# Compacting the heads' values by small transfers, and taking two groups of maxima ahead, in a decoder block

## The chip, the cores and the metric

The kernel runs on one core of a Trainium2 chip, as one launch. The metric is device time in microseconds (us), from the first to the last instruction and what lies around them. Matrix products run on TensorE (PE in the profile), vector work on VectorE (DVE), table functions and copies on ScalarE (ACT), some vector work on GpSimd (POOL); SyncE (SP) issues nearly all transfers.

## The reference

For four batches of 1024 tokens of width 256: self attention with 16 heads of width 16, whose queries and keys are made from 128-wide latents and rotated parts; a residual sum and layer norm; cross attention of the 1024 tokens with a context of 154 tokens under a mask; a residual sum and layer norm; then a routing layer with 8 experts of hidden width 512, each of which takes the best 256 tokens of every batch; last a layer norm. Cut to the attention and what follows it:

```python
attn = softmax(einsum('bhqd,bhkd->bhqk', query, key) / scale)
out = einsum('bhqk,bhkd->bhqd', attn, value)            # 16 heads of width 16
x = layernorm(x + out.transpose(0, 2, 1, 3).reshape(b, s, 256) @ Wo + bo)
# the same with the context as key and value, masked, W3 in Wo's place
x = layernorm(x + cross @ W3.T + b3)
probs = softmax(einsum('bsd,ed->bse', x, choice_w))     # 8 experts
```

## The kernel before

The time runs batch by batch. A batch has five stages: the self attention; its **out stage** (heads' values turned and divided, output projection, residual sum, layer norm, and then the query projection of the cross attention); the **operands** of the next batch's self attention; the **cross attention**; and its out stage, which ends in the logits of the routing (8 columns per token). A loop runs this body three times, and the fourth batch follows behind the loop without the parts for a next batch. The self attention of the first batch stands before the loop. After the fourth batch the experts run.

**Attention.** Heads go in groups of two, so there are eight groups. For each group three things happen. First the maxima: a product of 128 queries with all keys lands in two banks of PSUM and one VectorE reduction over it (`maximum`) gives the maximum. There are 16 of these per group of the self attention, 4 per group of the cross attention. GpSimd splits the negated maxima into three bfloat16 parts (`split_max`), PE turns them into rows (the order's step `turn`), ScalarE copies these (`nmT`), and SP moves them by three transfers into three extra rows of the queries' operand (`load_minus_max`). Second the scores (`st`): one product per 128 keys and 512 queries with keys in the rows, which subtracts the maximum through the extra rows, and one `Exp` on ScalarE. Third the weighted sum of values (`av`): up to four products side by side in one bank, four (head, half) pairs in 32 rows each. Column 17 of the values is 1, so row 16 of each 32 holds the sum of the exponentials. ScalarE copies the finished bank of a group into a slice of `oT`.

The order of these steps on every engine is a list written by `schedule` (`ORDER_SELF`, `ORDER_CROSS`, ...), one list for all engines: TensorE, VectorE and ScalarE each walk it and do their own part, in order. `ORDER_AHEAD` is the cross attention's list with the first 16 maxima of the next batch's self attention added (`ahead`, one after each `st` once the cross attention's own maxima are issued); `ORDER_NEXT` is the next self attention's list without them. The maxima use banks 0 to 3 in two pairs, so the product of one waits for the reduction two before it.

**The out stage** before: `o_tiles` turns `oT` (32 transposes), `heads_out` takes the reciprocal of the sums of every token and multiplies (8 reciprocals and 16 multiplications), `turn_heads` turns the result back (16 transposes) into `xT`, and `output` makes the projection (32 instructions, line L1568). `residual_sum` and `normalise` on VectorE, and a power on GpSimd, make the layer norm in two halves. In the self attention's out stage PE makes the `latents` of the next batch (L1409, 16 instructions) between the projection and the transposes of the normalised tokens (L1401); in the cross attention's it makes `context_values` (L1606 to L1616) there. `xTf`, the next batch's input, lies in the room of the keys before. Products that are copied out are handed on in a list of items (`Plan`), which also fixes their PSUM bank.

SP's program is a list too: in the loop's body it loads x, stores and reloads the split queries and keys, moves minus-maxima, and after the cross attention reloads the second half of the query stack, loads the mask, stores and reloads the context's parts, loads the residual and stores the normalised tokens (`x_rows`), before the next self attention's first minus-maxima.

## Time and profile before

| | us |
|---|---|
| median of 3 runs | 1962.59 (1958.56 to 1962.68) |
| the profiled execution | 1959.72 |
| its span | 1957.9 |

Busy over the span: PE 1668.1 us (85%), PE's weight loads 848.3, DVE 1134.5 (58%), ACT 891.8 (46%), POOL 429.8 (22%). The mean granted clock of TensorE was 0.907 of full speed.

How to read it: a row of the timeline has the start, the length, the engine, the source line, output and input by the program's names, the shape, and the count; in brackets behind it how long the engine had been idle and what released it. [...]

### The profile page before, as it was taken

The page shows a single profiled execution, that of the slowest core. Times are in us where ns is not written, and L with a number is a line of the kernel's source. Part 1 is how long each engine was busy: PE and PEld are TensorE (multiplying, and loading weights), DVE is VectorE, ACT ScalarE, POOL GpSimd, SP SyncE. Part 2 cuts the span into 40 slices and gives each one's busy share as a digit, 9 for nine tenths or more (in the row PEclk, how much of TensorE's full clock was granted, in tenths as well). Part 3 has the DMA queues.
Part 4 walks back from the last instruction along what each step waited for, and adds up shares of the span by engine and source line. Part 5 has one row for each costly group of instructions (what it writes and reads, how often), then busy time and mean ns, then how long its engine had stood idle before and what let it go on. Part 6 is the DMA issues. An engine that isn't in the chain of part 4 may idle for free. (4 is left out here: it accounts for less than half of the span.)

```text
span 1957.9 us, 32981 instructions
## 1 busy us (share of the span) xinstructions
PE 1668.1 (85%) x10632; PEld 848.3 (43%) x10632; DVE 1134.5 (58%) x1939; ACT 891.8 (46%) x1585; POOL 429.8 (22%) x547
## 2 busy tenths in 40 slices
PE   6599988798999888989998798999967844999993
PEld 3033334444332445433324354333245433888883
DVE  5577725756777256567763665677435366333424
ACT  2077773342777534347774343577833300111112
POOL 5200004302000052020001611100031001555563
PEclk9599999897999988979998899799988955999997
DMA  6700003622000044220000632200003040335446
GB/s 187 163 2 1 2 25 87 163 48 71 2 2 2 27 127 134 49 59 2 2 2 27 164 98 53 54 2 2 2 21 78 2 150 28 75 77 107 77 89 193
DMA packets 98037, 120.07 MB, mean 61 GB/s; under 512 B 17180, under 2 KB 73500, under 8 KB 97820
## 3 DMA queue, kind: packets, MB, share of 16 engines
q1 hardware_dynamic: 85468, 97.13, 18.1%
q0 software_dynamic: 12416, 20.98, 5.7%
q8 instruction: 86, 1.41, 0.3%
q14 instruction: 67, 0.55, 0.1%
HBM read 80.30 MB, written 40.79 MB: 62 GB/s over the span
## 5 line engine op out<-in xcount | busy, mean ns | idle before, releaser
L881 ACT ACTIVATE pT<-banks 128x512 f32<-128x512 f32 x1184 | 645.2, 596 | 254.8 <-PE banks L1492 150.0
L1034 DVE TENSOR_REDUCE nmf<-banks 128x1 f32<-128x1024 f32 x512 | 606.0, 1220 | 173.5 <-PE banks L1442 171.6
L1492 PE MATMUL banks<-qst,kst 99*128 99x512 bf16 x1024 | 344.0, 388 | 12.1 <-DVE nmf L1034 6.3
L1442 PE MATMUL banks<-kst,qst 96*128 96x512 bf16 x1024 | 327.0, 404 | 31.9 <-DMA kst<-k_parts 21.8
L1524 PE MATMUL banks<-pT,V 128*32 128x512 f32 x2048 | 273.8, 606 | 20.6 <-ACT oT L872 14.0
L1492 PEld LDWEIGHTS banks<-qst,kst 99*128 99x128 bf16 x1024 | 96.0, 97 | 307.2 <-ACT pT L881 185.8
L703 POOL CAST nmp<-nmf 128x16 bf16<-128x16 f32 x64 | 12.7, 198 | 831.4 <-DVE nmf L1034 516.6
L944 ACT ACTIVATE kst<-banks 128x512 f32<-128x512 f32 x64 | 38.2, 597 | 287.0 <-PE banks L1747 278.6
L1442 PEld LDWEIGHTS banks<-kst,qst 96*128 96x128 bf16 x1024 | 98.6, 100 | 146.4 <-DVE nmf L1034 37.3
L1029 DVE TENSOR_REDUCE nmf<-banks 128x4 f32<-128x616 f32 x128 | 99.6, 797 | 86.6 <-PE banks L1436 79.7
L1053 DVE RECIPROCAL rz<-banks 128x16 f32<-128x16 f32 x64 | 16.1, 251 | 204.5 <-PE banks L1552 203.4
L1277 DVE TENSOR_SCALAR kst<-banks,gate 128x256 f32<-128x256 f32 x64 | 28.0, 479 | 169.3 <-issue 164.6
L777 POOL DMA_INDIRECT acc_rows<-kst,tok_s x64 | 103.5, 1617 | 101.6 <-issue 97.7
L889 ACT ACTIVATE nmT<-banks 6x1024 bf16<-6x1024 bf16 x64 | 64.7, 1011 | 128.2 <-PE banks L1476 127.9
L1760 PE MATMUL banks<-qst,kst 128*128 128x256 f32 x512 | 120.8, 390 | 0.0
L1433 PE MATMUL banks<-maskb,identb 128*128 128x308 bf16 x256 | 79.3, 322 | 45.6 <-DVE V L1098 24.7
L1747 PE MATMUL banks<-kst,qst 128*128 128x256 f32 x512 | 117.9, 384 | 0.0
L1760 PEld LDWEIGHTS banks<-qst,kst 128*128 128x128 f32 x512 | 97.6, 194 | 12.9
L1747 PEld LDWEIGHTS banks<-kst,qst 128*128 128x128 f32 x512 | 96.5, 193 | 12.3
L1524 PEld LDWEIGHTS banks<-pT,V 128*32 128x32 f32 x2048 | 41.3, 108 | 132.3 <-ACT pT L881 131.3
L716 POOL TENSOR_TENSOR rstd<-ve,mhalf 128x4 f32<-128x4 f32 x16 | 16.3, 1018 | 331.0 <-DVE ve L1079 331.0
L770 POOL DMA_INDIRECT kst<-x_rows,tok_g x64 | 63.4, 991 | 88.7 <-DVE tok_s L1266 66.6
(176 smaller groups left out, 2016.7 us busy)
## 6 DMA issues: line engine op xcount, KB each, us to landing
qst<-q_parts SPq DMA_DIRECT2D x48, 256.0 KB, 5.2
kst<-k_parts SPq DMA_DIRECT2D x48, 256.0 KB, 3.8
qst<-in_w SPq DMA_DIRECT2D x16, 512.0 KB
q_parts<-kst SPq DMA_DIRECT2D x48, 128.0 KB, 2.5
k_parts<-kst SPq DMA_DIRECT2D x48, 128.0 KB, 3.9
qx_parts<-kst SPq DMA_DIRECT2D x48, 128.0 KB, 3.1
qxs<-qx_parts SPq DMA_DIRECT2D x24, 256.0 KB, 5.0
qst<-qx_parts SPq DMA_DIRECT2D x24, 256.0 KB, 4.9
```

Of the source, the lines that this page charges most:

```text
L770: pool.indirect_dma_start(xg[b][:, j, :], None, x2_rows, bass.IndirectOffsetOnAxis(tok_g[half][:, b, j:j + 1], 0)).then_inc(s_g[b], 16)
L777: pool.indirect_dma_start(acc_rows, bass.IndirectOffsetOnAxis(tok_s[half][:, b, j:j + 1], 0), yg[b][:, j, :], None, compute_op=ALU.add).th ...
L881: act.activation(pT[:, n % RING_P, :], PS[:, banks[what, n], :], ACT.Exp, scale=scale).then_inc(s_ex, 1)
L889: act.activation(nmT[:, m % 2, :], PS[0:3 * G, banks[what, n], :].bitcast(BF16), ACT.Copy).then_inc(s_ne, 1)
L1029: dve.tensor_reduce(nmf[:, m % 2, j, 4 * u:4 * u + 4].rearrange("p (a t) -> p a t", a=2), scores[:, :, 0:2 * SK].rearrange("p a (t k) -> p ...
L1034: dve.tensor_reduce(nmf[:, m % 2, j, t:t + 1], scores.rearrange("p a n -> p (a n)"), AX.X, ALU.max, negate=True).then_inc(s_smu, 1)
L1433: pe.matmul(ps[:, 0:2 * SK], identb[:, :], maskb[:, t0:t0 + 2, 0:SK], start=True, stop=False, skip_group_check=True)
L1442: ins = pe.matmul(pair[:, half, :], qst[0:KQ, h, t * P:(t + 1) * P], kst[0:KQ, h, half * N:(half + 1) * N], start=True, stop=True)
L1492: ins = pe.matmul(ps, kst[0:KM, head, kc * P:(kc + 1) * P], qst[0:KM, head, cols], start=True, stop=True)
L1524: ins = pe.matmul(av[V32 * j:V32 * (j + 1), :], Vf[:, kc, (g * G + j // HALVES) * VD:(g * G + j // HALVES) * VD + V32], pT[:, n % RING_P, ...
L1747: ins = pe.matmul(PS[:, 2 + 2 * k + f // 2, (f % 2) * CAP:(f % 2 + 1) * CAP], we1[half][:, c, f * P:(f + 1) * P], xgT[k][:, c, :], start=( ...
L1760: ins = pe.matmul(PS[:, 6 + k, j * D:(j + 1) * D], hT[k][:, f, j * P:(j + 1) * P], we2[half][:, f, :], start=(f == 0), stop=(f == F // P - 1))
```

## The change

Five things change.

1. ScalarE copies a group's bank into one of two slots (`avr`) instead of `oT`, and waits first until the slot's last content has been moved (`s_oc`). SP moves it (`compact`) by five transfers: the four rows of sums to `sums` (32 rows by 512), and four times 16 rows to their place in `xT`, which is already the layout that the projection wants. In the self attention a group's transfers stand two groups late in SP's list, in the cross attention four groups late; the last two (four) groups' stand behind its end.
2. The 32 + 16 transposes, 8 reciprocals and 16 multiplications of an out stage go. In their place (`divided`, `inverses`) one reciprocal of `sums` (32 x 512), four products with a matrix of ones and zeros (`spread`), which give every row of `xT` its inverse, and four multiplications of `xT` by the bank (128 x 512). `divided` waits first until the transfers of all eight groups have landed.
3. PE's `latents` and `context_values` move ahead of `inverses`, so ahead of the projection; `xTf` has its own room, and x is loaded earlier.
4. 32 maxima of the next batch are taken in the cross attention instead of 16: one after every second `st` from the fourth on while the cross attention's own maxima are issued, then one after each. The next self attention's list has 32 fewer than the full 128, and nmf, which holds the maxima, has four slots instead of two.
5. The final layer norm's rows and the mask get other rooms, since `oT` is gone.

The core of the diff:

```diff
-OUT_SELF = [("o", "D")] * T + [("oT", "DA"[n % 2]) for n in range(4)] + [("y", "D")] * 4
+OUT_SELF = [("bc", "D")] * 4 + [("y", "D")] * 4
...
-EACH = Plan(OUT_SELF + LATENTS + INTO_CROSS + OPERANDS, OUT_CROSS + CONTEXT + ROUTING)
+EACH = Plan(LATENTS + OUT_SELF + INTO_CROSS + OPERANDS, CONTEXT + OUT_CROSS + ROUTING)
...
-AHEAD = SM_SELF // NG
+AHEAD = 2 * SM_SELF // NG
...
+    what, unit = step
+    pending = ("smax", SM_CROSS - 1) not in ORDER_AHEAD
+    if what == "st" and ahead < AHEAD and (unit >= 3 and unit % 2 if pending else True):
         ORDER_AHEAD.append(("ahead", ahead))
         ahead += 1
+ORDER_AHEAD += [("ahead", n) for n in range(ahead, AHEAD)]
...
+            def compact(b, cross, g):
+
+                wait_apart(sp, s_ave, b * 2 * NG + (NG if cross else 0) + g + 1)
+                slot = avr[:, g % 2, :]
+                sp.dma_start(sums[TILES * g:TILES * (g + 1), :], slot[HD:P:V32, :]).then_inc(s_oc[g % 2], 16)
+                for j in range(TILES):
+                    (h, half), rows = (g * G + j // HALVES, j % HALVES), slice(V32 * j, V32 * j + HD)
+                    sp.dma_start(xT[h % 8 * HD:(h % 8 + 1) * HD, h // 8, half * N:(half + 1) * N],
+                                 slot[rows, :]).then_inc(s_oc[g % 2], 16)
...
+                    act.wait_ge(s_oc[k % 2], 80 * (b * NG + (NG // 2 if n0 else 0) + k // 2) + START)
+                    act.activation(avr[:, k % 2, :], PS[:, AV_BANK, :], ACT.Copy).then_inc(s_ave, 1)
...
+            def divided(at, b, name, cross):
+
+                for i in range(2):
+                    dve.wait_ge(s_oc[i], 80 * (b * NG + (NG if cross else NG // 2)) + START)
+                dve.reciprocal(sums[:, :], sums[:, :]).then_inc(s_rz, 1)
+                for n in range(4):
+                    idx, (half, c) = at.nth(name, n), divmod(n, 2)
+                    cols = slice(half * N, (half + 1) * N)
                     ready(at, idx)
+                    dve.tensor_tensor(xT[:, c, cols], xT[:, c, cols], PS[:, at.bank(idx), :],
+                                      ALU.mult).then_inc(s_evd, 1)
...
+            def inverses(at, b, name, cross):
+
+                pe.wait_ge(s_rz, b * 2 + (2 if cross else 1))
+                for n in range(4):
+                    half, c = divmod(n, 2)
+                    pe.matmul(item(at, at.nth(name, n)), spread[:, c, half, :], sums[:, :],
+                              start=True, stop=True).then_inc(s_item, 1)
...
                 at = Place(EACH if more else LAST, b)
-                o_tiles(at, "o", 0, T)
-                turn_heads(at, "o", "oT")
-                output(at, "oT", "y", wo)
                 if more:
                     latents(at, b + 1)
+                inverses(at, b, "bc", False)
+                output(at, "bc", "y", wo)
                 turn_normalised(at, b, "x1T", 0)
```

The order of the instructions on two engines shows what moved. On PE, where the loop's body begins (the self attention's out stage), the program had this order before; `ident` is the identity, `z` the tokens, `wdq` and `wdkv` the latents' weights:

```order
L1682 UNCONDITIONAL_BRANCH
L1552 MATMUL banks<-ident,oT 128x128 x32
L1364 ISA
L1388 MATMUL banks<-ident,z 128x128
```

and behind 15 more transposes of `z`:

```order
L1568 MATMUL banks<-wo,xT 128x256 x16
L1573 ISA
L1409 MATMUL banks<-kst,wdq 128x512 x4
L1409 MATMUL banks<-kst,wdkv 128x512 x4
L1364 REGISTER_ALU
L1399 ISA
L1401 MATMUL banks<-ident,z 128x128 x4
```

The same place in the changed program:

```order
L1691 UNCONDITIONAL_BRANCH
L1691 ISA
L1426 MATMUL banks<-xTf,wdq 128x512 x4
L1426 MATMUL banks<-xTf,wdkv 128x512 x4
L1565 ISA
L1568 MATMUL banks<-sums,spread 128x512 x4
L1395 ISA x2
L1578 MATMUL banks<-wo,xT 128x256 x8
L1395 REGISTER_ALU
L1578 MATMUL banks<-wo,xT 128x256 x8
L1416 ISA
L1418 MATMUL banks<-ident,z 128x128 x8
```

The latents stand first now, and nothing stands between the projection and the transposes of the normalised tokens any more.

On PE at the start of the next self attention, behind the logits (`wch`), before; `kst,qst` is a product for a maximum, `nmp` the turn of the minus-maxima, `qst,kst` a score:

```order
L1626 MATMUL banks<-wch,xT 128x8 x16
L1364 REGISTER_ALU
L1427 REGISTER_ALU
L1442 MATMUL banks<-kst,qst 128x512 x2
L1427 REGISTER_ALU
L1442 MATMUL banks<-kst,qst 128x512 x2
L1472 ISA
L1476 MATMUL banks<-identb,nmp 6x128 x8
L1427 REGISTER_ALU
L1442 MATMUL banks<-kst,qst 128x512 x2
```

and now:

```order
L1636 MATMUL banks<-wch,xT 128x8 x16
L1395 REGISTER_ALU
L1489 ISA
L1493 MATMUL banks<-identb,nmp 6x128 x8
L1501 ISA
L1503 ISA
L1509 MATMUL banks<-qst,kst 128x512 x2
```

Seven maxima stood ahead of the first score (two of them before the turn); none does now. On SP, behind the cross attention's last minus-maxima, the transfers of the last four groups now stand ahead of the reload of the query stack:

```order
L541 DMA kst<-onesb 3x128x128
L556 DMA sums<-avr 4x512
L559 DMA xT<-avr 16x512 x4
L556 DMA sums<-avr 4x512
L559 DMA xT<-avr 16x512 x4
L556 DMA sums<-avr 4x512
L559 DMA xT<-avr 16x512 x4
L556 DMA sums<-avr 4x512
L559 DMA xT<-avr 16x512 x4
L438 REGISTER_ALU
L517 DMA qst<-q_parts 16x8x1024 x6
```

Before, the reload came right behind the first of these rows.

## Rows read from the trace of the kernel before

**Rows 1.** Timeline, PE, out stage of the first self attention (start, length, engine)

```profile
287.95 5.35 PE L1552 MATMUL banks<-ident,oT 128*128 128x128 f32 x32 [1.21 <-ACT oT L872]
...
306.96 3.60 PE L1409 MATMUL banks<-kst,wdkv 128*128 128x512 f32 x8
...
312.31 7.13 PE L1409 MATMUL banks<-xT,w 128*128 128x512 f32 x16
```

**Rows 2.** Timeline, PE, the same stage in the loop's second turn

```profile
668.55 6.30 PE L1552 MATMUL banks<-ident,oT 128*128 128x128 f32 x32 [5.75 <-issue]
...
693.46 7.13 PE L1409 MATMUL banks<-xT,w 128*128 128x512 f32 x16
```

**Rows 3.** Timeline, ACT and PE, the same stage in the fourth batch, without latents

```profile
1426.88 0.60 ACT L872 ACTIVATE oT<-banks 128x512 f32<-128x512 f32 x1 [1.26 <-PE banks L1524]
...
1436.45 7.17 PE L1568 MATMUL banks<-wo,xT 128*128 128x256 f32 x32 [0.69 <-ACT xT L815]
...
1451.42 9.10 PE L1409 MATMUL banks<-xT,w 128*128 128x512 f32 x16
```

**Rows 4.** Busy time in three stretches: length, then each engine, PEclk, DMA, GB/s

```profile
288.20:291.60 3.40, 3.40 (x19) 3.40 (x18) 2.42 (x10) 0.00 (x0) 0.00 (x0) 0.50 0.55 209
...
668.50:673.90 5.40, 5.35 (x25) 5.38 (x26) 3.73 (x15) 0.00 (x0) 0.00 (x0) 0.50 0.01 3
...
1448.70:1455.60 6.90, 5.94 (x13) 3.45 (x14) 0.90 (x3) 1.71 (x3) 4.51 (x1) 0.51 0.00 0
```

**Rows 5.** Timeline, ACT and PE, out stages of first and last cross attention

```profile
433.65 0.60 ACT L872 ACTIVATE oT<-banks 128x512 f32<-128x512 f32 x1 [2.27 <-PE banks L1534]
...
442.34 7.17 PE L1568 MATMUL banks<-w,xT 128*128 128x256 f32 x32 [0.76 <-ACT xT L815]
...
459.78 6.99 PE L1626 MATMUL banks<-wch,xT 128*128 128x8 f32 x32 [0.76 <-ACT xT L815]
...
1554.02 7.17 PE L1568 MATMUL banks<-w,xT 128*128 128x256 f32 x32 [0.69 <-ACT xT L815]
...
1569.95 6.99 PE L1626 MATMUL banks<-wch,xT 128*128 128x8 f32 x32 [0.69 <-ACT xT L815]
```

**Rows 6.** Groups by line: the two kinds of reciprocal (min/median/max ns)

```profile
L1053 DVE RECIPROCAL rz<-banks x64: 246/248/259, 288.8 to 1551.7; 128x16 f32<-128x16 f32 x64
...
L1131 DVE RECIPROCAL lgm<-lgs x4: 202/202/205, 472.6 to 1578.1; 128x8 f32<-128x8 f32 x4
```

**Rows 7.** Timeline, SP and PE: three small transfers and who waited for them

```profile
94.60 1.90 SPq L513 DMA_DIRECT2D qst<-nmT  x3
...
97.74 1.01 PE L1492 MATMUL banks<-qst,kst 99*128 99x512 bf16 x2 [1.74 <-DMA qst<-nmT]
```

**Rows 8.** Timeline, SP and PE: start of the second self attention

```profile
471.42 25.16 SPq L513 DMA_DIRECT2D qst<-nmT  x6
...
476.58 1.06 PE L1492 MATMUL banks<-qst,kst 99*128 99x512 bf16 x2
```

**Rows 9.** Timeline, PE, self attention without maxima (281 on) and with (483 on)

```profile
281.53 1.06 PE L1524 MATMUL banks<-pT,V 128*32 128x512 f32 x8
...
283.60 1.07 PE L1524 MATMUL banks<-pT,V 128*32 128x512 f32 x8
...
483.70 1.07 PE L1524 MATMUL banks<-pT,V 128*32 128x512 f32 x8
...
486.54 1.06 PE L1524 MATMUL banks<-pT,V 128*32 128x512 f32 x8
```

**Rows 10.** Timeline, PE, cross attention: five `ahead` between the first two, none after

```profile
790.66 1.06 PE L1534 MATMUL banks<-pT,Vr 26*32 26x512 f32 x8
...
797.83 1.06 PE L1534 MATMUL banks<-pT,Vr 26*32 26x512 f32 x8
...
803.97 1.06 PE L1534 MATMUL banks<-pT,Vr 26*32 26x512 f32 x8
...
809.15 1.06 PE L1534 MATMUL banks<-pT,Vr 26*32 26x512 f32 x8
```

More of the change, by code:

```diff
@@ L410, in decoder_block @@
         s_ave = sem("values_taken")
+        s_oc = [sem(f"values_compacted{i}") for i in range(2)]
+        s_rz = sem("sums_inverted")
         s_z = sem("stats_ready")
@@ L551, in rest_of_batch @@
                     load_x(b + 1)
+                for g in range(NG - 2, NG):
+                    compact(b, False, g)
                 wait_apart(sp, s_qx[0], b * 96, s_qx[1], b * 96, s_ql[1], b * 96 + 96)
@@ L573, in rest_of_batch @@
                     load_minus_max(b, NG + g, cross_rows(g))
+                    if g >= 4:
+                        compact(b, True, g - 4)
                 if more:
                     load_ones()
+                for g in range(NG - 4, NG):
+                    compact(b, True, g)
+                if more:
                     at = Place(EACH, b)
@@ L670, in _ @@
             link(pool.memset(Vr[:, :, HD:HD + 1], 1.0))
+            link(pool.memset(spread[:, :, :, :], 0.0))
+            for c in range(C):
+                for half in range(HALVES):
+                    link(pool.affine_select(out=spread[:, c, half, :], in_=spread[:, c, half, :],
+                                            compare_op=ALU.not_equal, fill=1.0, base=-H * c - half,
+                                            pattern=[[-HALVES, P // HD], [0, HD]], channel_multiplier=1))
             link(pool.memset(kxst[:, :, :], 1.0))
@@ L693, in split, with split_max @@
                                            ALU.subtract).then_inc(s_p4, 1)
-            def split_max(b, n0, g0, sm_group, groups=range(NG)):
+            def split_max(b, base, what, g0, sm_group, places, groups=range(NG)):
                 for g in groups:
@@ L1061, in residual_sum, with maximum @@
-            def residual_sum(at, name, half, meanwhile=None):
+                        maximum(b + 1, base, places[what, n], 0, n, False, False)
+            def maximum(b, base, at, g0, n, cross, first):
+                made, pair = base + at, at % 2
+                sm_group = (SM_CROSS if cross else SM_SELF) // NG
+                g, k = divmod(n, sm_group)
+                m = g0 + g
+                if k == 0 and not (m < 4 and first):
+                    dve.wait_ge(s_nm, b * 2 * NG + m - 3)
+                dve.wait_ge(s_sm, made + 1)
+                scores = PS[:, 2 * pair:2 * pair + 2, :]
+                if cross:
+                    j, u = divmod(k, 2)
+                    dve.tensor_reduce(nmf[:, m % 4, j, 4 * u:4 * u + 4].rearrange("p (a t) -> p a t", a=2),
+                                      scores[:, :, 0:2 * SK].rearrange("p a (t k) -> p a t k", k=SK),
+                                      AX.X, ALU.max, negate=True).then_inc(s_smu, 1)
+                else:
+                    j, t = divmod(k, T)
+                    dve.tensor_reduce(nmf[:, m % 4, j, t:t + 1], scores.rearrange("p a n -> p (a n)"),
+                                      AX.X, ALU.max, negate=True).then_inc(s_smu, 1)
@@ L1411, in project, with maximum @@
                 ins.then_inc(s_item, 1)
-            def maximum(b, n0, n, cross):
+            def maximum(b, base, at, n, cross):
                 sm_group = (SM_CROSS if cross else SM_SELF) // NG
```

193 lines of the change are left out of this document (69 added, 124 removed).

## The prediction

> **What bounds the kernel now.** I read the busy shares first, then the timeline of PE stage by stage, then the groups by line for the operations that the change trades. PE is busy 85% of the span. Inside the attentions it is the pace: a weighted sum follows the last by 2.07 us in the self attention while no maxima are taken and by 2.84 us while two are taken per four scores [rows 9]; in the cross attention a group lasts 7.17 us with five `ahead` in it and 5.18 us without [rows 10]. So taking a maximum elsewhere saves and costs PE time, not only VectorE time. Between the attentions the out stages are chains: last copy by ScalarE, turn, division, turn, projection, layer norm, next projection or logits. From the last copy to the logits this takes 459.78 - 434.25 = 25.5 us [rows 5]. There are eight such stages.
>
> **Self attention's out stage, three times with latents.** In the first batch PE starts at 287.95 and reaches the query projection at 312.31, in the second at 668.55 and 693.46 [rows 1, 2]. The wait of 5.75 us ahead of the second start ends with "issue": PE comes round its loop there, and this stays. What goes are 48 transposes, and VectorE's reciprocals and multiplications beside them. What comes ahead of the projection is the latents (8 records in 3.60 us [rows 1], two such groups, overlapping: 7.0 us) and four products of 512 columns, which are again 8 records: 3.5 us. The latents used to cover the layer norm. How long projection to next projection takes with nothing in between is seen in the fourth batch: 1451.42 - 1436.45 = 15.0 us [rows 3]. So the changed stage takes 7.0 + 3.5 + 15.0 = 25.5 us from PE's start: 313.45 for 312.31 in the first batch (+1.1), 694.05 for 693.46 in the second (+0.6), and the third as the second. The transfers and the reciprocal lie under the latents here. If they did not, only what passes 7.0 us would count.
>
> **The stages without that cover: fourth self attention, four cross attentions.** From the last copy: SP issues five transfers. Three small ones took from 94.60 to 97.74 until PE went on, of which 1.90 is the issue [rows 7]; five at 0.4 to 0.6 us each plus the same landing make 3.4 to 4.4 us, and I take 3.9. Then the reciprocal of 512 values per row. The trace has 8 values in 202 ns and 16 in 248 [rows 6], 5.75 ns for each further value, which gives 0.20 + 504 x 0.00575 = 3.1 us. The two rows differ in their source too, so part of the 46 ns may be that; the floor is about 0.7 us, what VectorE needs if it makes one value as fast as it multiplies one. I take 2.5. PE's four products then take 3.5, and the projection starts 9.9 us after the copy. Before it started 1436.45 - 1427.48 = 9.0 us after it in the fourth self attention [rows 3] and 442.34 - 434.25 = 8.1 us in the cross attention [rows 5]. The multiplications by VectorE run beside the products. So +0.9 for the fourth self attention. In the cross attention of the loop `context_values` moves into the wait; projection to logits then takes what it takes in the last batch, 15.9 us for 17.4 [rows 5], so 9.9 + 15.9 = 25.8 for 25.5, +0.3 three times. The last cross attention has nothing to move: +1.8. Sum so far: 1.1 + 1.2 + 0.9 + 0.9 + 1.8 = 5.9 us.
>
> [...]
>
> **What the clock adds.** After waits of PE the granted clock stands at half: 3.4 us of it at 288.2, 5.4 us at 668.5 after the 5.75 us wait, and 6.9 us at 1448.7 behind the uncovered layer norm [rows 4], where the query projection then took 9.10 us for 7.13 [rows 1, 3]. Half speed loses half of the stretch when PE has products to stream. The transposes of before paid part of this too, and that is already inside the starting times above. So in the changed kernel: latents at half clock, 1.7 + 2 x 2.7 = 7.1; the query projection behind the layer norm, now uncovered in three more stages, 3 x 2.0 = 6.0; the `inverses` and the projection after a wait of 6 to 7 us with no work, 2.7 each in the fourth self and the last cross attention, and 1.7 in the three cross attentions where `context_values` shortens the wait to some 3 us, 10.5 together. Sum 23.6 us. The bounds are 0 and 30.
>
> **Maxima ahead.** Sixteen more in each of three cross attentions, at (7.17 - 5.18) / 5 = 0.40 us each: 6.4 us, less 1.0 for those at the end, where ScalarE and PE wait for each other (2.27 us before ScalarE's last copy [rows 5]). Were VectorE the bound there, each would cost what a maximum takes it, at most 2.84 / 2 = 1.42 us [rows 9]. In the next self attention seven maxima go from ahead of the first score and nine from between scores. The nine save (2.84 - 2.07) / 2 = 0.385 each, 3.5 us. The first score stands at 476.58, and the transfers that it needs were issued from 471.42 [rows 8]: 5.2 us, for 3.1 us in rows 7, as I read it because the megabyte store of the normalised tokens is issued just ahead of them. Without the two maxima ahead of the turn (1.9 us at the half clock, where two products of 512 columns take 1.06 [rows 8]) they are issued at 469.5, and SP has been through its context transfers earlier, because the context's products come earlier. So the first score comes at 469.5 + 3.1 = 472.6, 4.0 us earlier, of which I give back 1.0 as the clock is then low for more of the scores. Gain 6.5, cost 5.4, net -1.1 each time, -3.3 in all. The new slots of nmf take away short waits of VectorE that PE did not feel. The first `ahead` needs the next batch's first keys; their transfers are issued ahead of this point as before, and I cost that wait at nothing (at most one landing, the 3.1 us of rows 7, three times). The extra set-up of `spread` on GpSimd falls into its idle time at the start.
>
> **Sum.** 5.9 + 23.6 - 3.3 = 26.2 us on the profiled 1959.7 us: 1985.9, say 1986. That execution lies 2.9 us under the median and inside the runs' range, so no correction is made. The terms' bounds give 1970 to 2000 for this case.
>
> **Rivals.**
> - The clock does not fall where I put it. For it: in the cross attention's out stage PE now has work on both sides of a short wait. Against it: all three stretches of rows 4 follow waits of this size. Then 5.9 - 3.3 = +2.6: 1962.
> - Faster: the transfers and the reciprocal are short, so PE hardly waits. With issues of 0.4 us and a reciprocal of 0.7, `inverses` starts 4.2 us after the copy and the projection 7.7 us after it: fourth self attention -1.3, last cross -0.4, three cross stages -1.9 each; with +2.3 for the stages with latents and -3.3 for the maxima: -8.4, 1951, if the clock holds. It decides at the point where the projection starts earlier than 8.1 us after a cross attention's last copy. Against it stands the slope of rows 6.
> - The reciprocal is dearer per value than the slope of rows 6, whose two lengths are both far below 512. At one and a half times that slope, 8.6 ns, it takes 0.2 + 504 x 0.0086 = 4.5 us, 2.0 more than I took, in the five stages without cover: +10, 1996. [...]
> - VectorE bounds the `ahead` maxima, or they wait for keys: 1.42 - 0.40 = 1.0 us more for each of 48 is +49 at most; for the first seven of each cross attention alone, which share VectorE with the cross attention's own maxima, it is +21: 2007. For it: those seven. Against: in rows 10 five in a row cost PE 0.40 each.
>
> **How the numbers follow.** Forecast 0.55, clock stays 0.15, faster 0.12, slow reciprocal 0.12, VectorE or keys 0.06. A measurement of this kernel can tell about 0.2% from no change, 4 us. Faster: the second rival and a part of the first, 0.15. Same: the larger part of the first, 0.12. Slower: 0.73. The range leaves out the faster rival and half of the last: 1958 to 2002. The forecast's own is 1970 to 2000.
>
> **What would show it.** Right: latents directly behind the self attention, at half clock in part; a gap of PE of 3 us or more between `context_values` and the first product with `spread`; a reciprocal of 2 us or more; the projection 12 us or so after a cross attention's last copy; a second gap of some 3.5 us in the layer norm of all eight stages, with the clock at half after it; the first score some 6 us behind the logits; cross attentions longer by 5 to 6 us. Wrong: a granted clock that stays full in the out stages, a reciprocal under 1 us, or `ahead` steps that cost more or less than 0.4 us.

## The result and the profile after

The changed kernel takes 2042.17 us (median of 4 runs, 2035.79 to 2043.85), the kernel before 1960.57 us beside it: ratio 1.0413, 95% interval 1.0383 to 1.0443. It is 82 us slower, where 26 were forecast, and outside the predicted range of 1958 to 2002. The page's span and busy times read:

```profile
span 2039.4 us, 32497 instructions
PE 1671.1 (82%) x10312; PEld 823.2 (40%) x10312; DVE 1150.3 (56%) x1771; ACT 882.5 (43%) x1569; POOL 432.9 (21%) x552
```

PE is busy for about as long as before, in a longer span: the transposes are gone, but other products run longer (the mean granted clock fell from 0.907 to 0.888), and PE waits more. The list of PE's waits has what it waited for (us in total, times, longest). The first is for the layer norm's output, the second for the reciprocals; the third is for keys, of which 22.9 us are the kernel's start and the rest the next batch's keys at an `ahead`:

```profile
PE banks L1418 <- DVE z L1117: 64.6, 16, 11.7
PE banks L1568 <- DVE sums L1078: 32.7, 6, 9.7
PE banks L1459 <- DMA kst<-k_parts: 27.7, 4, 22.9
```

Cut into stages by events of the trace (us, summed over so many batches): "self out" runs from ScalarE's last copy to the query projection, "to cross" from there to VectorE's first maximum of the cross attention, "cross out" from the last copy to the logits, "to exp" from the logits to the next first exponential, "self att" from there to its last copy.

```
                 self out  to cross  cross att  cross out  last cross out  to exp  self att
                    x4        x4        x4         x3           x1           x3       x3
before            108.6     168.3     292.4       76.6         24.0         52.6    559.9
predicted after   121.6     174.3     308.6       82.6         28.5         43.6    549.4
after             123.5     170.2     317.5      127.2         33.3         40.7    555.3
```

Most columns are near. The three cross out stages of the loop are 50.6 us longer than before, for 6.0 predicted: that is where the prediction failed. Of the 56 us that the forecast lacked, 44.6 stand there, 8.9 in the cross attentions, 5.9 in the self attentions and 4.8 in the last cross out stage; smaller differences both ways make the rest.

The timeline of the first of these three stages, PE first (ScalarE's last copy ends at 448.24), answers [rows 5]:

```profile
451.54 1.09 PE L1626 MATMUL banks<-w2x,cxT 128*26 128x256 f32 x16
457.33 7.19 PE L1568 MATMUL banks<-sums,spread 32*128 32x512 f32 x8 [4.71 <-DVE sums L1078]
464.45 9.63 PE L1578 MATMUL banks<-w,xT 128*128 128x256 f32 x32
475.58 1.09 PE L1418 MATMUL banks<-ident,z 128*128 128x128 f32 x8 [1.50 <-DVE z L1117]
488.38 1.97 PE L1418 MATMUL banks<-ident,z 128*128 128x128 f32 x8 [11.71 <-DVE z L1117]
491.11 6.99 PE L1636 MATMUL banks<-wch,xT 128*128 128x8 f32 x32 [0.76 <-ACT xT L853]
504.03 3.38 PE L1509 MATMUL banks<-qst,kst 99*128 99x512 bf16 x7 [4.25 <-DMA qst<-nmT]
```

Each of the program's four `spread` products stands here as two records (x8), and each of the projection's 16 as two (x32). VectorE, GpSimd and SP in the same stretch:

```profile
452.72 1.19 DVE L1145 TENSOR_TENSOR Vr<-banks,brow 26x128 f32<-26x128 f32 x4 [0.65 <-PE banks L1626]
453.94 3.34 DVE L1078 RECIPROCAL sums<-sums 32x512 f32<-32x512 f32 x1
474.16 1.37 DVE L1117 TENSOR_SCALAR z<-z,mv,rstd 128x256 f32<-128x256 f32 x4
478.72 9.61 DVE L1117 TENSOR_SCALAR z<-z,mv,rstd 128x256 f32<-128x256 f32 x4 [1.12 <-POOL rstd L752]
...
478.66 4.38 POOL L762 TENSOR_SCALAR maskb<-mask_i 128x1232 bf16<-128x1232 int32 x1
483.02 4.51 POOL L757 TENSOR_TENSOR xb<-xb,brow 128x2048 f32<-128x2048 f32 x1
...
448.52 0.53 SPq L556 DMA_DIRECT2D sums<-avr  x1
449.09 2.40 SPq L559 DMA_DIRECT2D xT<-avr  x4
```

An SPq row is the issue and not the transfer: later in this stage the one of the tokens' megabyte store (`x_rows`) takes 0.41 us, and these stores land 4.5 us after their issue, the median of four.

The same four normalising operations take 1.37 us together for the first half of the tokens and 9.61 us for the second. The second four start 0.06 us after GpSimd's mask operation. One by one in the trace, the first of them takes 4.47 us and ends 0.15 us behind the mask operation (at 483.19), the next takes 4.58 us and ends 0.15 us behind the residual operation (at 487.68), and the other two take 0.40 us each. In the kernel before, VectorE's second four and GpSimd's two operations read

```profile
454.14 2.27 DVE L1085 TENSOR_SCALAR z<-z,mv,rstd 128x256 f32<-128x256 f32 x4 [1.12 <-POOL rstd L716]
...
456.23 4.41 POOL L726 TENSOR_SCALAR maskb<-oT 128x1232 bf16<-128x1232 int32 x1
...
474.09 4.50 POOL L721 TENSOR_TENSOR xb<-xb,brow 128x2048 f32<-128x2048 f32 x1 [13.45 <-DMA xb<-in_x]
```

because the split of the context's keys (two operations of some 0.8 us) stood between the layer norm's last factor (`rstd`) and the mask on GpSimd, and the residual operation waited for its load until 474.09. PE's granted clock in the changed kernel was this (columns as in [rows 4]; the clock is the third number from the end, 0.50 and 0.74 of full speed):

```profile
457.30:464.50 7.20, 7.17 (x9) 2.53 (x9) 2.06 (x3) 0.00 (x0) 0.00 (x0) 0.50 0.83 192
464.50:474.00 9.50, 9.50 (x33) 7.70 (x32) 5.26 (x15) 0.00 (x0) 1.02 (x1) 0.74 0.29 52
```

The `spread` products run wholly at half clock (0.50), the projection partly (a mean of 0.74). In the kernel before the clock stood at 1.00 from 434 to 449.6. In a self out stage with latents the `spread` products take 3.69 us:

```profile
287.55 3.69 PE L1426 MATMUL banks<-xTf,wdq 128*128 128x512 f32 x8 [1.23 <-ACT avr L909]
291.08 3.60 PE L1426 MATMUL banks<-xTf,wdkv 128*128 128x512 f32 x8
294.98 3.69 PE L1568 MATMUL banks<-sums,spread 32*128 32x512 f32 x8 [0.30 <-DVE sums L1078]
313.54 1.97 PE L1418 MATMUL banks<-ident,z 128*128 128x128 f32 x8 [3.49 <-DVE z L1117]
```

In the fourth self out stage and the last cross out stage, without latents or context products, they take 7.2 us behind waits of 8.65 and 9.65 us:

```profile
1503.66 7.19 PE L1568 MATMUL banks<-sums,spread 32*128 32x512 f32 x8 [8.65 <-DVE sums L1078]
1630.50 7.16 PE L1568 MATMUL banks<-sums,spread 32*128 32x512 f32 x8 [9.65 <-DVE sums L1078]
```

### The profile page after: what moved, and what is told of

Read it like the earlier page. It is cut to its first block and busy times, and to the rows that moved or that the text cites. A ratio compares the mean times of both kernels' runs of the same rounds, so it can differ in the third digit from the quotient of the medians.

```text
span 2039.4 us, 32497 instructions
## 1 busy us (share of the span) xinstructions
PE 1671.1 (82%) x10312; PEld 823.2 (40%) x10312; DVE 1150.3 (56%) x1771; ACT 882.5 (43%) x1569; POOL 432.9 (21%) x552
## 5 line engine op out<-in xcount | busy, mean ns | idle before, releaser
L1459 PE MATMUL banks<-kst,qst 96*128 96x512 bf16 x1024 | 316.8, 392 | 31.0 <-DMA kst<-k_parts 27.7
L1078 DVE RECIPROCAL sums<-sums 32x512 f32<-32x512 f32 x8 | 26.7, 3341 | 174.0 <-DMA xT<-avr 173.9
L853 ACT ACTIVATE xT<-banks 128x512 f32<-128x512 f32 x24 | 13.9, 596 | 220.4 <-PE banks L1418 220.4
```

The source lines that it names most:

```text
L1459: ins = pe.matmul(pair[:, half, :], qst[0:KQ, h, t * P:(t + 1) * P], kst[0:KQ, h, half * N:(half + 1) * N], start=True, stop=True)
```

## The experiments

The kernel before took 1952.0, 1959.9 and 1953.2 us in the three sets of runs, so ratios to it are compared; each heading has the ratio and its 95% interval. A ratio higher by 0.001, or 0.1 points, is 2 us. The changed kernel's own ratio is 1.0413. Times of stages come from one trace of each kernel. The stretch behind the last logits, which no experiment edits, took 379 to 388 us in these traces, so small differences of a stage are not read as effects.

### GpSimd's mask and residual held back (1.0318, 1.0301 to 1.0336)

```
 if more:
+    pool.wait_ge(s_ln, b * 2 * T + 2 * T)
     mask_bias(b + 1)
     residual(b + 1)
```

> The changed kernel, with GpSimd's mask and residual operations of the next batch held back until VectorE has normalised. Theory: these two operations slow VectorE's four normalising operations beside them (9.61 us for 1.37 in the trace after) and PE waits for those. Then each of three cross out stages gets 6 to 8 us shorter and the time comes to 2018 to 2024 us, with the four operations at 2.3 us or less. Rival 1: they were slow for another cause (transfers, the port to PSUM); then they stay near 9.6 us and the time is within 4 us of 2042. Rival 2: the contention only moves on to VectorE's copies and its reduction for the logits; then normalising is short, but the logits come less than 3 us earlier, 2034 or more.

Measured: 2014.9 us, a ratio 0.95 points lower, so some 18 us were won. Its first cross out stage, VectorE then GpSimd:

```profile
476.28 1.38 DVE L1118 TENSOR_SCALAR z<-z,mv,rstd 128x256 f32<-128x256 f32 x4 [1.12 <-POOL rstd L752]
477.58 0.68 DVE L1010 COPY xT<-banks 128x512 f32<-128x512 f32 x1
478.87 0.69 DVE L1010 COPY xT<-banks 128x512 f32<-128x512 f32 x1 [0.61 <-PE banks L1419]
...
477.91 4.38 POOL L762 TENSOR_SCALAR maskb<-mask_i 128x1232 bf16<-128x1232 int32 x1 [1.66 <-DVE z L1118]
```

The 9.61 us became 1.38, and the three stages are 24.4 us shorter in sum. VectorE's copies out of the banks keep their 0.68 us beside the same mask operation, and the logits come 8.1 us earlier, so both rivals fall and the theory stands. The self out stages are 4.7 us longer in sum. In the second of them PE waited as long as in the changed kernel (5.08 us for 5.09), but its clock did otherwise behind the wait: the projection ran at a granted clock of 0.73 and took 9.70 us, where it had 1.00 and 7.17 us. No run says why.

### Maxima placed as before, in the changed kernel (1.0426, 1.0408 to 1.0443)

```
-AHEAD = 2 * SM_SELF // NG
+AHEAD = SM_SELF // NG
-    if what == "st" and ahead < AHEAD and (unit >= 3 and unit % 2 if pending else True):
+    if what == "st" and ahead < AHEAD and not pending:
```

GpSimd's split follows, with one group ahead for two.

> The changed kernel with the maxima placed as before the change (one group ahead, none before the cross attention's own maxima are done); the compaction by transfers stays. Theory: the longer cross attentions (+25.1 us in the trace after) come from the maxima, and so does most of what came back (first exponential 11.9 us earlier in all, self attentions 4.6 shorter): the sum falls by 5 to 12 us, 2030 to 2037. By the prediction's own terms (maxima 0.40 us each ahead, 0.385 saved each, first score 3 us earlier) it would rise by 3.3, to 2045. Rival: the cross attentions are longer because of the copies and transfers of the compaction; then they stay near 82 us and the time rises by the lost gain of 4.6 to 16 us, to 2047 or more.

Measured: the intervals show no difference from 1.0413, so the theory's fall of 5 to 12 us did not come. The rise of 3.3 us by the prediction's own terms would fit, but is too small to be told from none. Stage by stage its parts are there: the cross attentions are 25.2 us shorter, the first exponential comes 11.7 us later in sum, and the self attentions take 7.8 us more. The rival, for which the cross attentions would have stayed long, falls. In the changed kernel the extra maxima pay for themselves, and no more is shown.

### The maxima alone, in the kernel before (1.0114, 1.0096 to 1.0133)

The edit is the fourth point of the change without the others: `AHEAD`, `ORDER_AHEAD`, `places`, four slots of `nmf`.

> The kernel before with only the second part of the change: maxima of the next batch's first two groups inside the cross attention, four slots for them; the heads' values leave the attention as before. Theory: the cross attentions get 8 us longer, the first exponential comes up to 3.9 us earlier and the self attention is up to 2.6 shorter, three times: 0.998 to 1.003 of before, as 1.0426 without and 1.0413 with these maxima in the changed kernel. By the prediction's terms it would be 3.3 us faster, 0.998. Rival: without VectorE's smaller load of the changed kernel the added maxima cost more; then 1.004 or above.

Measured: 22 us slower, so the rival's figure holds, but not for its reason. The cross attentions are 25.2 us longer, as in the changed kernel, so a maximum costs no more there. But nothing comes back: the stretch to the first exponential takes 18.2 us for 17.5, a self attention 186.9 for 186.6. PE and SP ahead of the first score:

```profile
485.62 3.37 PE L1503 MATMUL banks<-qst,kst 99*128 99x512 bf16 x7 [8.71 <-DMA qst<-nmT]
...
476.19 0.41 SPq L463 DMA_DIRECT2D xb<-in_x  x1
476.94 0.41 SPq L600 DMA_DIRECT2D x_rows<-z  x1
478.08 1.92 SPq L522 DMA_DIRECT2D qst<-nmT  x3
```

Three transfers, issued 1.1 us behind a megabyte's store and 1.9 us behind a megabyte's load, take 7.5 us until PE goes on. In the changed kernel store and load are 12 and 24 us back, and the same three take 3.1 us (500.95 to 504.03):

```profile
476.35 0.40 SPq L464 DMA_DIRECT2D xb<-in_x  x1
488.55 0.41 SPq L620 DMA_DIRECT2D x_rows<-z  x1
500.95 1.94 SPq L523 DMA_DIRECT2D qst<-nmT  x3
```

As I read it, the rest of the change lets the maxima earn their cost, because it moves the context's products and transfers ahead and leaves the queue empty at this point. Two traces agree with that; moving load and store alone beside these maxima was not tried.

### The division left out (1.0360, 1.0331 to 1.0389)

```
-dve.reciprocal(sums[:, :], sums[:, :]).then_inc(s_rz, 1)
+dve.tensor_copy(sums[:, :], sums[:, :]).then_inc(s_rz, 1)
```

> The changed kernel with the reciprocal of the 32 x 512 sums replaced by a copy of the same shape, so the division is left out. Theory: the reciprocal (3.34 us) stands on the path in the five stages without latents, and is hidden by the latents in three. With a copy at some 0.5 us each of the five gets 2.8 us shorter, and up to 1 us more where PE's clock has less time to fall: 2023 to 2028. Rival 1: something else comes as late (the transfers of the heads' rows, the context's products); then less than 1 us each, 2037 or more. Rival 2: it is on the path in all eight: 2015 to 2020.

Measured: 0.53 points lower, some 10 us. The copy takes 0.82 us, where the reciprocal took 3.34:

```profile
453.97 0.82 DVE L1078 COPY sums<-sums 32x512 f32<-32x512 f32 x1
454.85 6.26 PE L1568 MATMUL banks<-sums,spread 32*128 32x512 f32 x8 [2.19 <-DVE sums L1078]
```

The projections of the four cross out stages start 3.7 us earlier on average. In the first of them 2.5 us is the reciprocal and 0.9 shorter `spread` products. The fourth self out stage's projection starts 2.9 us earlier. So the theory's place is right, and its sum of 14 to 19 us is too large. The first rival (under 1 us each) is excluded, and so is the second: the three stages with latents are 1.1 us shorter in sum.

### PE kept busy in its waits (1.0357, 1.0339 to 1.0375)

```
+def keep_busy(at, idx, times):
+    for _ in range(times):
+        pe.matmul(item(at, idx), ident[:, :], cosT[:, 0:N], start=True, stop=True)
...
+if cross or at.plan is LAST:
+    keep_busy(at, at.nth(name), 4)
 pe.wait_ge(s_rz, b * 2 + (2 if cross else 1))
...
+if k == 0:
+    keep_busy(at, idx, 3)
 if chunk == 0:
     pe.wait_ge(s_ln, ...)
```

> The changed kernel with products of no use (identity by 512 columns of the cosine table, into the bank that the next real product overwrites) where PE waits: four ahead of the `spread` products in the four cross out stages and in the last self out stage, three ahead of the turn of the normalised tokens in all eight. Theory: PE's clock falls to half in these waits, and the products behind them pay for it (the four `spread` products 7.19 us for 3.5, the query projection 9.0 for 7.1). Kept busy, the clock stays up: 3 to 5 us less in each of five stages, 1.5 to 2.5 in each of three, 2016 to 2027. Rival: the waits are filled but the clock stays low, or the products start late and push the real ones back; then 2038 to 2050.

Measured: 0.56 points lower, some 11 us, where 15 or more were expected.

```profile
445.73 3.70 PE L1411 MATMUL banks<-cosT,ident 128*128 128x512 f32 x8
450.51 3.82 PE L1576 MATMUL banks<-sums,spread 32*128 32x512 f32 x8 [1.08 <-DVE sums L1078]
454.26 8.69 PE L1586 MATMUL banks<-w,xT 128*128 128x256 f32 x32
```

The `spread` products take 3.82 us for 7.19, at a granted clock of 0.95 for 0.50, with nothing changed but what PE did in the wait: the clock is the cause. The projection behind them got only part of it (8.69 us, clock 0.82). The loop's cross out stages are 3.8 us shorter each, as expected. The self out stages won nothing in sum. One of them became 6.0 us longer: PE started 1.5 us later behind the loop's turn (the jump back to the loop's start), and its projection ran at a clock of 0.73, 9.70 us for 7.17.

### All three taken away (1.0082, 1.0064 to 1.0101)

This has GpSimd held back and PE kept busy as above, and the reciprocal waits for the sums' transfers alone and stands ahead of `context_values` on VectorE:

```
+s_os = [sem(f"sums_compacted{i}") for i in range(2)]
...
+inverted(b, True)
 if more:
     context_values(at)
 divided(at, b, "bcx", True)
```

> The changed kernel with GpSimd's mask and residual operations held back, PE kept busy in the waits as before, and the reciprocal started as soon as the sums are there (their transfer has a semaphore of its own, and the reciprocal stands ahead of the context's values on VectorE). Theory: the three causes add up, 17 us for the contention, 12 for the clock, and 1 to 2 us in each of five stages for the earlier reciprocal: ratio 1.010 to 1.017 against the kernel before. What is then left is the out stage by transfers itself: a wait of 6 us at least between the last copy and the first `spread` product, where the turns of before worked. Rival: contention and clock cover each other (PE waits less for VectorE, so there is less clock to win) and the ratio stays at 1.022 or above. Other rival: at 1.005 or below the compaction itself costs nothing and all of the loss was side effects.

Measured: 1.0082, a little better than the theory's 1.010 to 1.017, whose lower end the interval just reaches. Two of the loop's cross out stages take 26.7 us, for 42.4 in the changed kernel and 25.5 before. The third takes 30.9, with a projection at a clock of 0.72 after all. The reciprocal now starts 2.2 us after the last copy, for 5.7. So the causes do not cover each other: 33 of the 41 thousandths of the loss go away without undoing the change. The rival of 1.022 falls, and the one of 1.005 too. All four cross out stages together are 46.1 us shorter than in the changed kernel; the first two edits alone gave 24.0 and 12.9, which leaves some 9 for the earlier reciprocal, which was not run alone. The self out stages are 6.3 us shorter here, where the single edits made them 4.7 and 1.9 longer; that is not explained, and it is part of why the gain is larger than the single ones in sum.

### And the maxima as before too (1.0061, 1.0047 to 1.0076)

> The changed kernel with the three causes taken away as in the last such run and also the maxima placed as before, so only the compaction by transfers stays of the change. Theory: 8.4 us less in each cross attention, 3.9 more until the first exponential and 0 to 2 more in the self attention: 7 to 12 us less than the 1.0082 of that run, ratio 1.002 to 1.005. Rival: the maxima cost nothing in all, as 1.0426 without and 1.0413 with them say for the changed kernel as it was; then 1.008 to 1.009 again.

Measured: 1.0061. Its interval overlaps that of 1.0082, so no difference between the two is shown; it takes in the theory's upper end of 1.005, and the rival's 1.008 lies just outside. What is left, 12 us, is what the compaction costs less what the products of no use bring. By stages against before: self out +6.8 us, the loop's cross out +6.4, last cross out +6.2, and to cross -7.8, where the clock was kept up.

### The exclusion by itself, in the kernel before (1.0090, 1.0075 to 1.0105)

```
 if more:
+    mask_bias(b + 1)
     split(b + 1, 8, 9)
-    mask_bias(b + 1)
     residual(b + 1)
```

> The kernel before with one edit: GpSimd's mask operation goes ahead of its split of the context's keys, directly behind the layer norm's second rstd. Theory: it then starts together with VectorE's four normalising operations, which read and write SBUF and wait until GpSimd's operation has ended: they take 4.4 us or more in place of 1.4 to 2.3, and PE's turns wait for them. The logits come 2.5 to 4 us later three times, ratio 1.004 to 1.006. Rival: no exclusion between the two engines, the 9.61 us of the changed kernel had another cause (its transfers, its bank reads); then within 0.1% of before.

Measured: one line moved made the kernel some 17 us slower, more than the 8 to 12 us of the theory's ratio.

```profile
453.21 5.88 DVE L1085 TENSOR_SCALAR z<-z,mv,rstd 128x256 f32<-128x256 f32 x4 [1.12 <-POOL rstd L716]
...
453.15 4.38 POOL L726 TENSOR_SCALAR maskb<-oT 128x1232 bf16<-128x1232 int32 x1
```

The first of the four ends 0.15 us behind GpSimd's operation, which ends at 457.53. The logits come 3.6 us later in each batch of the loop, as expected, 10.8 us in sum. Of the rest, 2.7 us in sum stand between logits and first exponential and 4.1 in the self attentions; these are not explained. The rival, no exclusion between the two engines, falls.

### The store behind the maxima's transfers, in the kernel before (1.0034, 1.0020 to 1.0047)

```
 load_minus_max(b, g, qst[:, g * G:(g + 1) * G, :])
+if g == 0 and not isinstance(b, int):
+    store_normalised(b - 1)
```

The store's place ahead of the self attention is gone.

> The kernel before with one edit: SP's store of the normalised tokens goes behind the transfers of the first group's maxima, which PE waits for. Theory: those took 5.2 us in the trace before because the megabyte store was issued just ahead, and 3.1 us on a quiet queue; so 1.5 to 2.5 us less in each of three turns, ratio 0.996 to 0.998. Rival: they were slow because of the keys' and masks' transfers, or SP comes to them no earlier; then within 0.1% of before.

Measured: 7 us slower, which neither the theory nor the rival had. In the first batch the first exponential comes exactly as before, 17.47 us behind the logits, so the store was not what it waited for. PE's products ahead of it wait for VectorE, which has ten maxima and the experts' softmax to do. In the second batch this stands there, and in the third the same operation takes 4.10 us:

```profile
854.72 0.20 DVE L1137 RECIPROCAL lgm<-lgs 128x8 f32<-128x8 f32 x1
855.07 4.33 DVE L1138 TENSOR_TENSOR prob<-lge,lgm 128x64 f32 x1
859.52 3.58 DVE L1040 TENSOR_REDUCE nmf<-banks 128x1 f32<-128x1024 f32 x3
...
854.83 4.49 POOL L727 TENSOR_TENSOR xb<-xb,brow 128x2048 f32<-128x2048 f32 x1 [12.10 <-DMA xb<-in_x]
```

An operation of 0.23 us (`prob`) takes 4.33 us, until GpSimd's has ended at 859.32. In the kernel before, the residual operation starts 1.1 us behind this one; in the first batch here it starts 0.06 us behind it, and the operation keeps its 0.23 us; in the second it starts 0.24 us ahead. Maxima out of the banks run beside the same GpSimd operation at their 1.18 us (four in 4.71 us from 473.75 in the first batch).

### PE kept busy in the kernel before (1.0031, 1.0020 to 1.0042)

This has the edit of the run before, three products of no use in the layer norm's waits where no latents stand, and five ahead of the first score.

> The kernel before with that edit and with products of no use on PE in the layer norm's wait of the four cross out stages and of the last self out stage (three) and ahead of each self attention's first score (five). Theory: the clock falls in these waits in the kernel before as well, 2 to 3.5 us lie in the scores behind the first and 1 us in the turns and logits: with the moved store ratio 0.991 to 0.995. Rival: the clock falls in spite of them, or they end after the wait they fill and delay the scores: 0.997 or more.

Measured: the mean clock rises from 0.907 to 0.921, and the time does not fall; with the moved store alone the ratio was 1.0034. The first exponential comes 20.1 us behind the logits in all three batches, for 17.5 in the kernel before: the five products end after the wait that they fill. The last cross attention starts 2.1 us earlier. The rival's second form holds.

### Context transfers late, softmax later, in the kernel before (0.9982, 0.9971 to 0.9993)

```
-wait_apart(sp, s_kx, b * 192 + 192)
-load_context(b + 1)
...
 load_minus_max(b, g, qst[:, g * G:(g + 1) * G, :])
+if g == 0 and not isinstance(b, int):
+    wait_apart(sp, s_kx, b * 192)
+    load_context(b)
...
-if order is ORDER_NEXT and n == AHEAD + 3:
+if order is ORDER_NEXT and n == AHEAD + 19:
```

> The kernel before with two edits: SP issues the next batch's context transfers (three stores and twelve loads) behind the transfers of the first group's maxima, so that the residual is loaded and used earlier, and VectorE's softmax of the experts stands 16 maxima later. Theory: between logits and first score VectorE is the chain in the kernel before (ten maxima of 1.18 us and the 0.9 us of that softmax), so 0.9 us go, three times, and the risk that GpSimd's residual operation holds up that softmax with them: ratio 0.998 to 0.999. Rival: the transfers of the first maxima end that wait, and a quiet queue gives 2 us more each: 0.996 to 0.997. Other rival: the residual operation now meets the layer norm, 1.002 or above.

Measured: as the theory has it. The first exponential comes 16.61 us behind the logits for 17.5, earlier by the softmax's 0.9.

### A version that beats both: four more maxima ahead (0.9928, 0.9914 to 0.9942)

This has the edits of the run before, with `AHEAD = SM_SELF // NG + 4`, all twenty maxima behind the cross attention's own, and three products of no use in the layer norm of the last self out stage.

> The kernel before with the edits of the third of these runs, with four more maxima ahead (20 for 16, all behind the cross attention's own maxima, where one costs PE some 0.4 us), and with PE kept busy in the layer norm's wait of the last self out stage. Theory: four maxima of 1.18 us less ahead of the first score bring it down to where the transfers bound it, up to 3.9 us earlier, for 1.5 to 2 us in the cross attention, three times, and 2.5 us in the last self out stage: ratio 0.994 to 0.997, faster than both kernels. Rival: as with the maxima alone, the transfers take 7 to 8 us here and nothing comes back: 1.000 to 1.003.

Measured: 1939.4 us for 1953.2, a little better than the theory's 0.994 to 0.997.

```profile
472.00 1.03 PE L1510 MATMUL banks<-qst,kst 99*128 99x512 bf16 x2 [0.93 <-DMA qst<-nmT]
...
451.51 0.39 SPq L463 DMA_DIRECT2D xb<-in_x  x1
456.40 0.41 SPq L601 DMA_DIRECT2D x_rows<-z  x1
468.91 1.94 SPq L522 DMA_DIRECT2D qst<-nmT  x3
```

With load and store 17 and 13 us back the transfers take 3.1 us (468.91 to 472.00), and the first exponential comes 13.5 us behind the logits, as in the changed kernel, for 1.5 us in each cross attention in place of 8.4. The self attentions are 2.3 us longer each and the stretches to the cross attention 1.8 us shorter each; neither is explained.

## Why the prediction was wrong

The direction and several mechanisms were right, and the sum was 56 us short: one mechanism was missing, and several terms were too small. By the prediction's own steps:

- **Cross out stages, +0.3 us each and 1.7 for the clock: the failed step.** The stages measured +16.9 each. The prediction counted projection to logits as in the last batch, 15.9 us, though there GpSimd has no next batch to prepare, and so put what GpSimd does beside VectorE at nothing. Here the stretch took 26.7 us. 8.2 us of this (9.61 less 1.38) is VectorE's normalising held up by GpSimd's mask and residual operations: the change takes the split of the context's keys from between `rstd` and the mask, and the residual is there early. The experiment that holds them back takes 8.1 us a stage away again, and one moved line in the kernel before brings 3.6 in. The prediction looked at what came sooner by the reordering, not at what would now run side by side. The traces show how: the operations that were held up (4.47 and 4.58 us for 0.40 here, 4.33 for 0.23 in the run with the moved store) start behind GpSimd's and end 0.08 to 0.15 us behind them. Copies (0.68 us) and maxima (1.18 us) out of the banks are untouched. Neither is everything outside the banks held up: the reciprocal of the first cross out stage starts 0.22 us into a GpSimd operation of 0.77 us (453.72) and takes its 3.34 us. No run shows which property of an operation decides it.
- **Its clock term there, 1.7 us, was too small.** `spread` at 7.19 us for 3.6 and the projection at 9.63 for 7.17 [rows 5] make 6.0 us. Filling the wait gave 3.4 us of it back.
- **Start of the `spread` products, 6.4 us after the copy.** It was 9.1. Transfers and reciprocal were sized at 3.9 and 2.5 us. The reciprocal took 3.34 us, between the prediction's floor of 0.7 and its dear rival's 4.5, and a third more than I took; from [rows 6] to this, each further value takes 6.2 ns. The transfers took 4.5 us from the copy in the fourth self out stage, where nothing covers them. In the loop's cross out stages VectorE's `context_values`, which I had counted only as filling, stood ahead of the reciprocal until 453.9, another 1.2. The three points together, 8.2 for the normalising, 4.3 for the clock (6.0 less 1.7) and 2.7 for the start (9.1 less 6.4), make up the 14.9 us a stage that the forecast lacked, within 0.3.
- **Self out stages, +13.0 with their clock: +14.9.** The latents cover transfers and reciprocal as predicted (PE waited 0.30 us in the first stage): +7.3 us for +9.4 in three stages. The fourth cost 7.6 us for 3.6, from the two causes above. The 6.0 us for a query projection at half clock were right for its own length (9.0 us for 7.1), but the stretch "to cross" grew by only 1.9 us in sum.
- **Last cross out, +4.5: +9.3.** PE waited 9.65 us (the transfers took 5.5 us here), and `spread` and projection began at half clock, so the projection started 16.1 us after the copy for 8.1 before.
- **Maxima in the cross attention, +5.4 each: +8.4.** Group by group it is 1.5 us in the second group and 1.5 and 2.0 in the sixth and seventh, 5.0 in all, for eleven maxima. The other 3.4 us stand in the first group, which now holds four `ahead`: at 0.40 us each they would be 1.6, and PE waits 1.3 to 2.0 us for the next batch's keys in front of the first of them. The prediction costed this wait at nothing, as their transfers are issued ahead of this point; they were issued, not landed. In the first batch:

```profile
386.22 0.60 PE L1459 MATMUL banks<-kst,qst 96*128 96x512 bf16 x2 [1.96 <-DMA kst<-k_parts]
```

- **First score 4.0 us earlier: 3.9, for a wrong reason.** I put [rows 8] down to the store ahead of the transfers. The moved store gave nothing in the first batch, and in the changed kernel with the maxima as before the store was 14 us back and the first exponential came 17.5 us behind the logits all the same. So VectorE's maxima ended that wait; they left with the change, and only then do transfers bound it, 3.1 us.
- **Nine maxima, -3.5 us each time:** it was -1.5. The whole difference stands in the first group. PE waits 0.5 us for ScalarE there now, and the granted clock was 0.61 over the 7 us from 505, for 0.78 over 6.4 us at this point before (476.6 to 483), which by these figures is an estimated 1.3 us more.
- **The rivals.** "Clock stays up" and "faster" fell with the half clock under `spread`. "Reciprocal dearer" had the right operation, with 4.5 us for the measured 3.34. "Keys bound the aheads" was partly true. None had the exclusion between the engines.
- **The range.** The clock term's own lower bound of 0 gives 1962 us, not the 1970 that the forecast's range starts at. The upper side was the one that failed: it had no term for two engines in each other's way. The signs named for being right (a wait ahead of `spread`, half clock behind it, a reciprocal above 2 us) nearly all came; none of them looked at VectorE beside GpSimd.

Open: in the second and third self out stage PE's first product behind the loop's turn comes after an idle time of 4.7 to 6.5 us that the profile puts to "issue", and the projection starts 16.1 to 20.2 us behind the last copy over the kernels with the compaction. Part of the spread is the clock: behind nearly equal waits the projection took 7.17 us at a granted clock of 1.00 in one trace and 9.70 us at 0.73 in another. No run was made on this, and it blurs the sums by some 4 to 6 us. After the last logits the changed kernel is 3.4 us shorter than the one before, which is inside the spread of that stretch over the traces.

## What to carry to other kernels

When a change moves an operation of GpSimd, list what VectorE runs beside its new place, and time each of it there: here normalising operations of 0.40 us took 4.47 and 4.58, while a reciprocal beside one of 0.77 us kept its 3.34 us, and a copy out of the banks beside the mask operation its 0.68. Taking away something that stood between two engines can cost as much as what is added: 8.2 us a stage here. Price a wait of PE as the wait and the half clock behind it: 4.71 us and then 7.19 for 3.6 in the first cross out stage. Products of no use took 3.4 us off the `spread` products there, but where five of them ended after the wait, the first exponential came 2.6 us later (20.1 for 17.5). Work moved ahead pays only down to the next limit, here transfers of 3.1 us with load and store 12 us back or more: to the first score four maxima, with the experts' softmax out of the way, gave what sixteen gave (13.5 us from the logits), at a fifth of the cost (1.5 us for 8.4).

## What was not expected of the hardware

- GpSimd held VectorE up: beside GpSimd's 4.38 us mask operation one normalising operation of 0.40 us took 4.47, and one of 0.23 us took 4.33 beside the residual operation (4.49 us), while operations of VectorE with an operand from the banks kept their times beside these two (0.41 us for `Vx`, 0.68 for a copy, 1.18 for a maximum).
- The reciprocal's time went with its values per row: 202 ns for 128 x 8, 248 ns for 128 x 16 and 3.34 us for 32 x 512, where a copy of that last shape takes 0.82 us.
- Three transfers of a few KB took 7.5 us in the trace where a megabyte's load and store were issued within 2 us ahead of them, and 3.1 us in two where these were 12 us back or more.
- Four products of no use, 0.92 us each, in a wait of 4.7 us brought the clock of the products behind it from 0.50 to 0.95.
